# Local layers' q, k and v projections as three one-pass products of split operands, with one set of value buffers for both layers

## The reference

```
xn = layernorm(x)
x + attention(xn) + local(xn)

attention: 16 heads of 64, causal; qkv = xn @ W_qkv + b; softmax; @ W_out + b
local: two layers, 8 heads of 64, each
  h = shift_token(x);  q, k, v = split(h @ wqkv[l])          # 128 -> 3 * 512
  q, k = rotary(l2norm(q) * qs, l2norm(k) * ks)
  x = x + softmax over the own and the previous block of 64 (q, k, v) @ wo
  x = x + (a * gelu(g)) @ w2,   a, g = split(layernorm(shift_token(x)) @ w1)
```

## Time and profile before

| | |
|---|---|
| median of 3 runs | 2740.16 us (2738.8 to 2740.53) |
| profiled execution, its own time | 2738.27 us |
| its span (first to last instruction) | 2736.5 us |
| PE busy | 2656.3 us, 97% |
| DVE, ACT, POOL busy | 70%, 61%, 42% |
| granted TensorE clock, mean | 0.991 |

### The profile page before, as it was taken

The page is one execution under the profiler, slowest core; times in us unless marked ns, Lnnn a source line. Parts: engine busy times, 40 slices in busy tenths (PEclk is TensorE's granted clock), DMA queues, the critical chain, the costliest instruction groups (busy, mean ns, idle before and its releaser), DMA issues.

```text
span 2736.5 us, 89709 instructions
## 1 busy us (share of the span) xinstructions
PE 2656.3 (97%) x34304; PEld 1821.8 (67%) x34304; DVE 1928.7 (70%) x7102; ACT 1656.7 (61%) x3030; POOL 1147.0 (42%) x1136
## 2 busy tenths in 40 slices
PE   2999999999999999999999999999999999999998
PEld 1667575766767677676766757667676776767665
DVE  2677776867677676776867668676776867768664
ACT  2575756557575665756657565565756647566564
POOL 3463725418063370814509054280633608145040
PEclk6999999999999999999999999999999999999999
DMA  4000000000000000000000000000000000000000
GB/s 108 2 9 3 5 11 2 6 10 6 10 6 3 9 6 10 6 3 9 6 10 6 11 1 7 10 6 10 5 3 9 6 10 6 6 6 10 2 10 6
DMA packets 41727, 25.17 MB, mean 9 GB/s; under 512 B 13042, under 2 KB 40540, under 8 KB 41308
## 3 DMA queue, kind: packets, MB, share of 16 engines
q1 hardware_dynamic: 41308, 19.43, 2.5%
HBM read 14.96 MB, written 4.19 MB: 7 GB/s over the span
## 4 chain that ended last, share of the span: by engine, by line
PE 87%; DVE 7%; issue 3%; POOL 1%; SPq 1%; ACT 0%; DMA 0%; DVEq 0%; POOLq 0%; ACTq 0%
PE bank L1307 12%; PE bank L1226 12%; PE bank L1145 10%; PE bank L1271 9%; PE bank L1298 4%; PE bank L1321 4%; PE bank L1282 4%; PE bank L1253 4%; PE bank L1332 3%; PE bank L1343 3%; PE bank L1138 3%; PE bank L1337 3%; PE bank L1140 3%; PE bank L1139 3%; PE bank L1186 3%
## 5 line engine op out<-in xcount | busy, mean ns | idle before, releaser
L1012 DVE CUSTOM_DVE_ANT_0 bank<-bank,future 128x128 f32<-128x128 f32 (+3 forms) x1024 | 475.9, 523 | 160.1 <-PE bank L1186 156.8
L806 POOL TENSOR_TENSOR lrstd<-lvar,minus_half 128x4 f32<-128x4 f32 x32 | 32.2, 1007 | 1274.4 <-DVE lvar L969 1274.4
L816 POOL TENSOR_TENSOR rnorm<-ssc,minus_half 128x8 f32<-128x8 f32 x256 | 431.4, 1685 | 21.3
L887 ACT ACTIVATE probs<-bank 128x512 f32<-128x512 f32 (+1 forms) x768 | 347.3, 535 | 135.3 <-PE bank L1235 134.5
L1226 PE MATMUL bank<-Qa,Ka 64*128 64x512 f32 (+3 forms) x2048 | 389.5, 460 | 5.8 <-DVE Oa L1042 3.3
L819 POOL TENSOR_TENSOR turn_a<-turn_a,turn_b 128x512 f32<-128x512 f32 x256 | 325.3, 1274 | 138.5 <-DVE turn_b L1067 138.2
L1307 PE MATMUL bank<-Lqkv,resid 128*128 128x512 f32 x768 | 367.9, 599 | 2.7 <-ACT resid L911 1.9
L1027 DVE CUSTOM_DVE_ANT_0 bank<-bank,band 128x192 f32<-128x192 f32 x1024 | 332.7, 394 | 26.9 <-PE bank L1203 26.6
L1271 PEld LDWEIGHTS bank<-Va,probs 128*64 128x64 f32 x10240 | 310.0, 138 | 26.4 <-issue 24.5
L1271 PE MATMUL bank<-Va,probs 128*64 128x65 f32 x10240 | 325.4, 223 | 1.0 <-DVE negf L1027 0.3
L895 ACT ACTIVATE lprobs<-bank 128x512 f32<-128x512 f32 x256 | 138.9, 595 | 305.6 <-PE bank L1258 305.6
(11 more groups left out here) (150 smaller groups left out, 6052.4 us busy)
## 6 DMA issues: line engine op xcount, KB each, us to landing
x_res<-in_L_attn_x SPq DMA_DIRECT2D x16, 256.0 KB, 2.9
x_rows<-in_L_attn_x SPq DMA_DIRECT2D x16, 256.0 KB, 4.5
out<-yT SPq DMA_DIRECT2D x16, 256.0 KB, 2.3
Lqkv<-in_L_ffn_wqkv SPq DMA_DIRECT2D x2, 768.0 KB, 4.6
rope_t<-in_rope SPq DMA_DIRECT2D x8, 128.0 KB, 4.8
Kf<-in_L_attn_W_qkv SPq DMA_DIRECT2D x1, 768.0 KB, 7.4
Qf<-in_L_attn_W_qkv SPq DMA_DIRECT2D x1, 768.0 KB, 8.8
Lw<-in_L_ffn_w SPq DMA_DIRECT2D x2, 341.0 KB
```

The lines of the kernel that those rows point to most:

```text
L816: g.tensor_tensor(rnorm[s][:, :], ssc[s][:, :], minus_half[:, :], ALU.pow).then_inc(rnorm_ready.sem, 1)
L887: psum.raise_read(a.activation(probs[j][:, at:at + n], psum.bank(scores, j)[:, 0:n], ACT.Exp, scale=float(HEAD) ** -0.5), scores, j)
L1012: ins = v.tensor_tensor_reduce(bank[:, at:at + n], bank[:, at:at + n], future[:, SEQ - n:SEQ], 1.0, -3.0e38, ALU.add, ALU.max, neg[p % 2][ ...
```

## The change

Each projection of the local layers is made by the helper `product`: three `float32r` matmuls of a high and a low part of both operands, in place of one float32 matmul. For that:

- `wqkv[l]` is loaded into buffers that are free at the start (`Kf[0]` for layer 0, `ff` in three loads for layer 1) and split once into `Lqkv[l]` high (three copies on ACT) and low (three subtractions on DVE), task `lsplit`. The first `f_rows` of the program, which writes into `ff[0]`, waits for layer 1's split.
- What enters a layer is split for every image and layer into one pair of buffers `entering`, task `resid`: one copy on ACT (waits for `f_first` or `f_down`, and until the layer before in `LAYERS` has made its last projection), one subtraction on DVE. The projections wait for the latter.
- `Vf` and `V_turned` exist once for both layers. The copy of a layer's `f_v` waits for the last `f_pv` of the layer before it in `LAYERS`, so of the other layer.
- Three memsets of POOL fall away. The table of costs, the offsets and the shifts are others, and so is the whole order.

```diff
+    "lsplit": dict(hi=(1.5, 1.6), lo=(1.85, 1.95)), "resid": dict(hi=(0.49, 0.6), lo=(0.6, 0.69)),
...
-    "f_q": dict(pe=(0.86, 0.92), square=(0.49, 0.6), turn=(1.27, 1.35), sum=(0.59, 0.67), add=(1.27, 1.3), pow=(2.0, 2.05), mult=(1.04, 1.1)),
+    "f_q": dict(pe=(0.72, 0.8), square=(0.49, 0.6), turn=(1.27, 1.35), sum=(0.59, 0.67), add=(1.27, 1.3), pow=(2.0, 2.05), mult=(1.04, 1.1)),
...
+        free = [layer(i, l, 1, kind, "pe", t) for kind in ("f_q", "f_k", "f_v") for t in range(TILES)]
+        yield part(("resid", l), "hi", [*entered, *free])
+        yield part(("resid", l), "lo", [of("resid", "hi"), *free])
+        entered = [of("resid", "lo")] + [here(("lsplit", l), "lo")] * first
...
-            free = [image(i - 1, ("f_pv", l, LPAIRS - 1, 1), "pe")]
-            yield part(task, "pe", entered + [here(("dma", "wqkv"), "in")] * first, 1, begun=free)
...
-OFFSETS = (0.0, 1.1, 0.878, 1.12)
-LAG, WASTE, SWITCH = 0, 1069.2, 0
+OFFSETS = (0.0, 1.107, 0.886, 1.128)
+LAG, WASTE, SWITCH = 0.37, 519.2, 1.8
...
-        Lqkv = [sb(f"Lqkv{l}", [P, 3 * INNER]) for l in range(DEPTH)]
+        Lqkv = [[sb(f"Lqkv{l}_{s}", [P, 3 * INNER], F32R) for s in ("hi", "lo")] for l in range(DEPTH)]
...
+        entering = [sb(f"entering_{s}", [P, SEQ], F32R) for s in ("hi", "lo")]
...
-        Vf = [sb(f"Vf{l}", [P, TILES, LHEADS, HEAD + 1]) for l in range(DEPTH)]
-        V_turned = [sb(f"V_turned{l}", [P, TILES, LHEADS, HEAD + 1]) for l in range(DEPTH)]
+        Vf = sb("Vf", [P, TILES, LHEADS, HEAD + 1])
+        V_turned = sb("V_turned", [P, TILES, LHEADS, HEAD + 1])
...
+        raw = [[Kf[0][:, c, :] for c in range(3)], [part[:, :] for part in ff]]
...
-            sp.dma_start(Lqkv[0][:, :], wqkv[0]).then_inc(whole_qkv[0], 16)
+            sp.dma_start(Kf[0][:, 0:3, :].rearrange("p c n -> p (c n)"), wqkv[0]).then_inc(whole_qkv[0], 16)
...
-            sp.dma_start(Lqkv[1][:, :], wqkv[1]).then_inc(whole_qkv[1], 16)
+            for c in range(3):
+                sp.dma_start(ff[c][:, :], wqkv[1][:, c * INNER:(c + 1) * INNER]).then_inc(whole_qkv[1], 16)
...
-                for part in V_turned:
-                    const(g.memset(part[:, 0, :, :], 0.0))
-                    const(g.memset(part[:, :, :, HEAD:HEAD + 1], 1.0))
+                const(g.memset(V_turned[:, 0, :, :], 0.0))
+                const(g.memset(V_turned[:, :, :, HEAD:HEAD + 1], 1.0))
...
+                elif kind == "lsplit":
+                    l = task[1]
+                    act.wait_ge(whole_qkv[l], 16 + 32 * l)
+                    for c in range(3):
+                        at = slice(c * INNER, (c + 1) * INNER)
+                        ins = a.activation(Lqkv[l][0][:, at], raw[l][c], ACT.Copy)
+                    ins.then_inc(layer_hi, 1)
+                elif kind == "resid":
+                    l = task[1]
+                    if l == 0:
+                        psum.wait_read(act, (i, ("f_first",), "pe"))
+                    else:
+                        psum.wait_read(act, (i, ("f_down", 0), "pe"))
+                    if TURN[i, l] > 0:
+                        used = last_of(layer(i, l, 1, k, "pe", t) for k in ("f_q", "f_k", "f_v") for t in range(TILES))
+                        psum.wait_filled(act, used)
+                    a.activation(entering[0][:, :], resid[l][:, 0:SEQ], ACT.Copy).then_inc(entering_high.sem, 1)
                 elif kind == "xt":
...
-                    psum.wait_filled(act, image(i - 1, ("f_pv", l, LPAIRS - 1, 1), "pe"))
+                    psum.wait_filled(act, layer(i, l, 1, "f_pv", "pe", LPAIRS - 1, 1))
...
+                elif kind == "lsplit":
+                    l = task[1]
+                    dve.wait_ge(layer_hi, l + 1)
+                    for c in range(3):
+                        at = slice(c * INNER, (c + 1) * INNER)
+                        ins = v.tensor_tensor(Lqkv[l][1][:, at], raw[l][c], Lqkv[l][0][:, at].bitcast(F32), ALU.subtract)
+                    ins.then_inc(layer_lo, 1)
+                elif kind == "resid":
+                    l = task[1]
+                    entering_high.wait(dve, (i, task, "hi"))
+                    v.tensor_tensor(entering[1][:, :], resid[l][:, 0:SEQ], entering[0][:, :].bitcast(F32),
+                                    ALU.subtract).then_inc(entering_low.sem, 1)
...
+                    if i == 0:
+                        dve.wait_ge(layer_lo, 2)
...
-                        pe.wait_ge(whole_qkv[l], 16)
-                    entered = (i, ("f_first",), "pe") if l == 0 else (i, ("f_down", 0), "pe")
-                    bank, = psum.claim(pe, here, [(entered, 0)])
+                        pe.wait_ge(layer_lo, l + 1)
+                    entering_low.wait(pe, (i, ("resid", l), "lo"))
+                    bank, = psum.claim(pe, here)
                     c = "qkv".index(kind[2])
-                    psum.raise_filled(mm(bank[:, :], resid[l][:, tile(t)], Lqkv[l][:, c * INNER:(c + 1) * INNER], start=True, stop=True), here)
+                    psum.raise_filled(product(bank[:, :], [part[:, tile(t)] for part in entering],
+                                              [w[:, c * INNER:(c + 1) * INNER] for w in Lqkv[l]]), here)
                 elif kind in ("f_qt", "f_kt"):
```

More of the change, by code:

```diff
@@ L265, in parts_of_image @@
             task = ("f_v", l, t)
-            free = [image(i - 1, ("f_pv", l, LPAIRS - 1, 1), "pe")]
-            yield part(task, "pe", entered + [here(("dma", "wqkv"), "in")] * first, 1, begun=free)
+            free = [layer(i, l, 1, "f_pv", "pe", LPAIRS - 1, 1)]
+            yield part(task, "pe", entered, 1, begun=free)
             yield part(task, "out", [here(task, "pe"), *free] + const, gives=[here(task, "pe")])
@@ L294, in parts_of_image @@
         yield part(("f_rows", l), "pow", [of("f_rows", "stats")])
-        yield part(("f_rows", l), "scale", [of("f_rows", "pow"), *free], gives=[of("f_rows", "pe")])
+        yield part(("f_rows", l), "scale", [of("f_rows", "pow"), *free] + [here(("lsplit", 1), "lo")] * first, gives=[of("f_rows", "pe")])
         yield part(("f_back", l), "pe", [of("f_rows", "scale")], 1)
@@ new lines @@
+    ("split", "hi"): -26.6, ("split", "lo"): 0.8, ("lsplit", "hi"): 7.4, ("lsplit", "lo"): 5.6, ("tables", "turn"): -7.7, ("norm", "stats"):
+    -4.7, ("norm", "pow"): 2.9, ("xt", "pe"): -22.3, ("xt", "lo"): 32.4, ("a_v", "pe"): 10.4, ("a_v", "out"): 20.8, ("a_proj", "q"): -3.0,
+    ("a_proj", "q_out"): -45.9, ("a_proj", "k"): 7.5, ("a_proj", "k_out"): 32.0, ("a_max", "pe"): 0.4, ("a_max", "max"): -7.6, ("a_neg", "pe"):
+    -1.8, ("a_neg", "out"): 32.6, ("a_st", "pe"): -0.5, ("a_st", "exp"): 6.6, ("a_pv", "pe"): -2.2, ("a_pv", "out"): 2.7, ("a_ot", "pe"): 18.4,
@@ new lines @@
+    ("a_ot", "out"): -1.3, ("a_out", "pe"): -5.4, ("a_out", "sum"): -12.5, ("out", "sum"): 30.6, ("out", "pe"): 26.6, ("out", "out"): -0.1,
+    ("f_first", "pe"): -1.8, ("f_first", "out"): -7.0, ("resid", "hi"): -21.3, ("resid", "lo"): 0.7, ("f_q", "pe"): 1.6, ("f_q", "turn"): 1.3,
+    ("f_q", "sum"): 1.3, ("f_q", "add"): -10.8, ("f_q", "pow"): -4.2, ("f_q", "mult"): 0.6, ("f_qt", "pe"): 1.1, ("f_qt", "out"): 47.5, ("f_k",
+    "pe"): 0.7, ("f_k", "turn"): -0.1, ("f_k", "add"): -0.2, ("f_k", "mult"): 5.0, ("f_kt", "pe"): -0.6, ("f_kt", "out"): -4.7, ("f_max", "pe"):
@@ L429 @@
+    -13.9, ("f_max", "max"): -2.5, ("f_neg", "pe"): 0.8, ("f_neg", "out"): -8.4, ("f_st", "pe"): -6.0, ("f_st", "exp"): -43.7, ("f_pv", "pe"):
+    3.9, ("f_pv", "out"): -39.1, ("f_ot", "pe"): 0.3, ("f_ot", "out"): -4.8, ("f_wo", "pe"): -21.9, ("f_wo", "add"): 23.7, ("f_rows", "pe"):
+    -0.7, ("f_rows", "pow"): -2.2, ("f_rows", "scale"): 0.2, ("f_back", "out"): -14.2, ("f_gate", "pe"): -4.6, ("f_up", "pe"): 7.9, ("f_up",
+    "mult"): -0.4, ("f_down", "pe"): -26.2, ("f_down", "add"): -0.9}
 ORDER, SLOTS, SPAN = in_order(PARTS, due_times(PARTS, OFFSETS, LAG, NUDGE), WASTE, SWITCH)
@@ L784, in make_rest @@
                     const(g.memset(Va[b][:, :, :, HEAD:HEAD + 1], 1.0))
[L785 to L786 removed]
+                const(g.memset(Vf[:, :, :, HEAD:HEAD + 1], 1.0))
                 for b in range(2):
```

25 lines of the change are left out of this document (15 added, 10 removed).

## The result

The changed kernel takes 2713.6 us (median of 4 runs, 2712.8 to 2714.3), the kernel before 2739.5 in the same measurement: ratio 0.991, 95% interval 0.989 to 0.992. It is 25.8 us faster; the forecast was 2701, 12.6 us lower.

A forecast was written before the change was run, and what follows sets the result against it. PE's work was taken to bound about 2670 us, a load the first 64. Span 2736.5 - 62.7 + 13.8 + 10 + 0 = 2697.6, with execution and median offsets of 1.8 and 1.9: 2701 us, range 2686 to 2724.

The forecast's parts named there:

- products: Local layers' projections on PE: 384 products go from 0.858 to 0.695 us each, 62.7 us less.
- 138 changes of tiling: PE's new list: 919 changes of tiling become 1057, at 0.10 us each, 13.8 us more.
- new waits: Steady periods: waits from the splits and shared value buffers, 10 us taken, between 0 and 34.
- start (and end): Start of the kernel: moved splits, rotary table and loads cost 0, with 2 us either way.
- a saving of a quarter: Rival on the local projections: the product costs a quarter less, saving 82.4 us, 2681 us; chance 4%.
- The rival in which the product isn't cheaper: Local projections: stationary loads could set the pace, product stays at 0.858 us, 2764 us; chance 3%.
- Its two covers: PE work before layer 1's first projection and first f_pv hides the 1.3 us split chain and 6.6 us of value copies.
- failed covers: Rival at layer 1: covers fail or DVE runs behind, waits of 34 to 43 us, 2725 to 2734; chance 8%.
- the value buffers as the bound: Rival at ACT's block of value copies: PE stands up to 4.5 us an image, 2759 us; chance 5%.
- the 42 to 46 given: Start of the kernel: PE's wait for Wqkv_lo would still be 42 to 46 us.
- the 3 that it named as a sign of being wrong: Start of the kernel: a start that moved by more than 3 us would show the prediction wrong.
- the 162 to 164: Steady period of one image: 162 to 164 us with PE idle 1 to 2; over 165 would be wrong.

The follow-up runs named there:

- e1: Operations of the kernel before, with two sets of value buffers, in the changed kernel's order of every engine's list: 2762.3 us, ratio to before 1.0085.
- e2: e1 with one set of value buffers for both layers: 2760.5 us, 1.8 less than e1.
- e3: The changed kernel with one float32 matmul of the high parts in place of each local projection's three passes, low parts left out: 2763.7 us.
- e5: As e4, but the added matmul works on 64 of the 128 rows, 480 changes of tiling more than e4: 2774.0 us.
- e6: As e4, but the added matmul fills 64 of the 128 columns, 480 changes of tiling more than e4: 2778.4 us.
- e7: The changed kernel without each local projection's third pass (high tokens by low weights), 384 passes less: 2658.4 us, 55.2 less than the changed kernel.
- e4: The changed kernel with 240 more small full-size matmuls amid the transposes of f_qt and f_kt, no change of tiling added: 2721.3 us.

## Why the prediction was right in kind and 12.6 us short

In steps of the medians: before to e1 +23.8 (order), e1 to e2 -1.8 (shared buffers), e2 to e3 +3.2 (splits), e3 to after -50.1 (products). They add up to -24.9 and not to -25.8, because after was measured beside another set of runs of before (2739.5 against 2738.5). By the terms of the forecast, the last three as estimates:

| term | forecast | measured |
|---|---|---|
| products | -62.7 | -60.8 |
| 138 changes of tiling | +13.8 | +17 to +18 |
| new waits | +10 | about +14 |
| start (and end) | 0 | about +4 |

**Products.** Right. 0.858 was confirmed by e3, whose chain shows eight projections in one piece of 6.87 us (0.859 each); 0.695 was read from two products and is 0.700 over nine, which is where the 1.9 us are. The Trainium skill, page "FP8 and Floating Point Precision", section "TensorE Precision Notes", has a true float32 product as four passes. By an estimate from that, three of them would take 0.644, and the measured 0.700 speaks against a saving of a quarter. The rival in which the product isn't cheaper falls too.

**Changes of tiling.** The term was mis-sized by 3 to 4 us. Its 0.10 was the way into a small tile; the bounds, 0.09 to 0.10, left the way back out. e5 and e6 give 0.124 and 0.13 on the mean of both ways, 17 to 18 us for 138. That takes their price for all kinds; changes between two kinds of small tile, and to and from the 64 by 64 tiles of `f_st`, were not measured by themselves. The Trainium skill, page "TensorEngine Tiling (Array Packing)", section "Key Properties", states that a change of tiling mode drains the engine, without a price. That both ways cost something here agrees.

**New waits.** Too small by about 4. Waits, start and end together come to about 18: 6 that are left of e1's 23.8 when the changes of tiling are taken off, 1.4 for shared buffers and splits together, and 10.6 from the table under e3. Some 4 of these belong to the start and the end (below). And the step sought the waits in the wrong place. Its two covers, in front of the first projections and of the first `f_pv` of layer 1, both held, so the rivals with failed covers or with the value buffers as the bound fall (2725 to 2759 against 2713.6). What the step left out is waits away from the new dependences: the one in front of `a_proj`, which came with the order, and those under e3, where work on PE that was shortened stood ahead of inputs from DVE and ACT that come no sooner than before. A steady period with 0.76 us of idle time does not say that there are microseconds of slack in front of each next input. That the 6 us left of e1 are waits is argued from its idle time (+4.9) and not shown apart: its repeated waits, 6.6 and 3.1, stand against 4.0 and 3.3 that the kernel before has at other places. That the time stayed well inside the range, with three terms too small, is partly luck: the upper bound allows 34 us for two covers, and these held.

**Start.** The wait came as forecast, the cost did not. The one long wait is two, 38.6 + 6.6 = 45.2, inside the 42 to 46 given. But ten steady periods, from the end of layer 1's `f_down` in image 2 to that in image 12, take 1658.5 us before and 1640.6 after. At sixteen of each that is 28.5 us won, and the span fell by 24.4: some 4 us are lost outside the steady part. In the first 260 us the splits cost 4.6 (e3 minus e2), and sharing the buffers gave 1.5 back (e2 minus e1): net about 3, past the forecast's 2 either way and at the 3 that it named as a sign of being wrong. Part of the loss is TensorE's clock, which the forecast has in none of its terms. Busy us by stretch as in the earlier trace rows, before and then after:

```profile
64.00:100.00 36.00, 33.09 (x310) 23.18 (x311) 24.07 (x79) 23.37 (x44) 33.19 (x31) 0.93 0.01 2
```

```profile
64.00:100.00 36.00, 30.28 (x255) 21.87 (x254) 26.46 (x68) 19.09 (x36) 31.18 (x29) 0.80 0.00 1
234.00:238.60 4.60, 2.68 (x32) 1.53 (x32) 4.60 (x30) 4.31 (x9) 0.00 (x0) 1.00 0.00 2
238.60:242.00 3.40, 3.36 (x8) 1.82 (x9) 2.51 (x16) 1.45 (x3) 0.00 (x0) 0.50 0.02 5
```

Before, the granted clock is at full speed (2.4 GHz) from 68.8 us on, up to the last few microseconds. After, it falls to the lower level (1.2 GHz) again from 74.7 to 78.2, from 81.6 to 88.4 and from 238.6 to 242.0, the last time behind 4.6 us of which PE worked 2.68. An `f_wo` falls into that stretch; after, and then e2, where the clock stays up there:

```profile
239.04 5.12 PE L1366 MATMUL bank<-Qf,Lwo 128*128 128x512 f32 x8
```

```profile
238.99 3.65 PE L1328 MATMUL bank<-Qf,Lwo 128*128 128x512 f32 x8
```

That is about 1.5 of the 4 us; how the rest divides between clock and waits is not shown.

The period, 164.2 in the stretch shown and 164.06 on the mean of the ten, is at the upper edge of the 162 to 164, PE's idle time in it within the 1 to 2.

The misses add up: 1.9 + 3.7 + 4 + 4 = 13.6, against 12.6.

## What to carry to other kernels

When a change alters operations and a planned order at once, run the old operations in the new order: it splits the result cleanly, and here the order took back 24 of the 49 us that the operations brought. Don't book an operation's saving at full price because its engine is 97% busy: ask at each place what the next task waits for, and by how little that input is early today. Price a switch of mode both ways, there and back. Compare sixteen steady periods with the span: what is left over lies in the start and the end, and there look at the clock too.

## What the runs showed of the hardware

A small matmul of another tiling between full tiles costs PE 0.247 us (64 rows) or 0.26 us (64 columns) more than one of the full size, which itself took 0.06. A pass of 128 by 128 by 512 in `float32r` took 0.233 us, a float32 matmul of that shape 0.859, 3.7 such passes. With the granted clock at its lower level for 3.4 us, eight records of an `f_wo` took 5.12 us in place of 3.65. A microsecond of PE work taken out of a list that is 97% busy was worth 0.82 us (e3 to after, 50.1 of 60.8) and, in the next step, 0.62 (e7, 55.2 of 88.5); in e4 a microsecond added cost 0.52.
